# Expert weights split on ScalarE and VectorE, router logits inside attention, one register load per sorted tile, weights moved in 2 KB pieces

## The reference

```python
x = _layernorm(x + attn(x))                  # 16 heads of 16, ONE k and v head of 16, causal
x = _layernorm(x + xattn(x, ctx, ctx))       # 32 query heads and 8 k/v heads of 8, not causal
probs = softmax(xf @ gate_w)                 # xf: 2048 x 256, 8 experts
w, idx = top_k(probs, 2); w = w / w.sum(-1)
out = sum over e of comb[:, e] * ((silu(g_e) * u_e) @ expert_down[e])   # g_e, u_e = xf @ expert_gate_up[e], 512 each
x = _layernorm(x + out + base_mlp(x))        # the base MLP has the same shape and runs on every token
```

## Time and profile before

| | us |
|---|---|
| median of 3 runs | 762.73 (762.64 to 770.33) |
| the profiled execution, whole | 764.03 |
| its span, first to last instruction | 762.2 (granted clock 0.957) |

### The profile page before, as it was taken

How to read it: one execution, slowest core, us unless ns; L and a number is a source line. 1 busy time by engine, 2 the same in 40 slices (tenths; PEclk the granted TensorE clock), 3 DMA queues, 4 the chain that set the end, 5 groups by cost and what they waited for, 6 DMA issues and landing times. The chain is left out here.

```text
span 762.2 us, 11308 instructions
## 1 busy us (share of the span) xinstructions
PE 632.4 (83%) x3379; PEld 436.6 (57%) x3379; DVE 476.9 (63%) x972; ACT 307.3 (40%) x657; POOL 224.8 (29%) x223
## 2 busy tenths in 40 slices
PE   3767989898898898899767998997898888998981
PEld 2444435555454545454335876776686776777770
DVE  4578998988888988978762472333333333344286
ACT  2435656655656655565553211222222222223114
POOL 2344653244432244423200002233333333332100
PEclk9989999999999999999997799999999999999997
DMA  8241344413444313342204800015515542110513
GB/s 265 84 152 59 138 138 153 150 65 105 152 139 153 130 65 124 138 145 105 90 14 149 374 0 28 29 53 197 210 42 201 208 152 92 44 47 24 183 39 110
DMA packets 34727, 90.46 MB, mean 119 GB/s; under 512 B 6028, under 2 KB 24975, under 8 KB 33648
## 3 DMA queue, kind: packets, MB, share of 16 engines
q1 hardware_dynamic: 30928, 80.43, 29.5%
q0 software_dynamic: 3744, 9.31, 3.8%
HBM read 56.18 MB, written 34.47 MB: 119 GB/s over the span
## 5 line engine op out<-in xcount | busy, mean ns | idle before, releaser
L1135 ACT ACTIVATE silu<-inner 128x512 f32<-128x512 f32 x55 | 32.9, 598 | 185.4 <-PE inner L1523 135.1
L493 ACT ACTIVATE prob<-scores 128x1024 f32<-128x1024 f32 x96 | 98.2, 1025 | 13.1 <-PE scores L846 7.8
L1296 DVE TENSOR_TENSOR hT<-hiddenT,hT 128x512 fp32r<-128x512 f32 x39 | 27.0, 692 | 111.5 <-ACT hT L1141 111.5
L1113 POOL DMA_INDIRECT chosen_y<-y_rows,to_row x39 | 40.0, 1026 | 161.2 <-DVE y_rows L1311 161.2
L1518 PE MATMUL inner<-weights,sT_hi 128*128 x156 | 69.1, 443 | 20.9 <-issue 20.9
L626 DVE TENSOR_REDUCE max_c<-scores 128x8 f32<-128x1024 f32 x64 | 77.9, 1217 | 5.8 <-PE scores L909 4.3
L919 PE MATMUL scores<-q_c,k_c 128*128 128x512 f32 x128 | 48.0, 458 | 33.3 <-DVE max_s L626 26.9
L390 POOL TENSOR_TENSOR xT_lo<-xT_in,xT_hi 128x256 fp32r<-128x256 f32 x16 | 11.9, 747 | 192.5 <-ACT xT_hi L464 192.5
L1107 POOL DMA_INDIRECT rows<-x,from_row x39 | 38.1, 978 | 91.9 <-DVE from_row L1278 80.4
L933 PE MATMUL sums<-prob,v_c 128*32 128x512 f32 x256 | 63.0, 604 | 0.0
L1519 PE MATMUL inner<-weights,sT_hi 128*128 x156 | 61.8, 396 | 0.0
(11 more groups left out here) (217 smaller groups left out, 1482.1 us busy)
## 6 DMA issues: line engine op xcount, KB each, us to landing
split_w<-halves SPq DMA_DIRECT2D x16, 1536.0 KB, 6.6
weights<-split_w SPq DMA_DIRECT2D x8, 3072.0 KB, 11.2
raw_w<-in_expert_w SPq DMA_DIRECT2D x16, 768.0 KB, 8.1
weights<-chosen_y SPq DMA_DIRECT2D x8, 512.0 KB, 7.4
xT_in<-in_xT SPq DMA_DIRECT2D x16, 128.0 KB, 2.7
x_in<-in_x SPq DMA_DIRECT2D x16, 128.0 KB, 2.4
x<-stream SPq DMA_DIRECT2D x16, 128.0 KB, 1.7
ctxT_in<-in_ctxT SPq DMA_DIRECT2D x16, 96.0 KB, 2.3
```

The lines of the kernel that those rows point to most:

```text
L493: act.activation(prob[:, m, :], scores[:, n, :], ACT.Exp, scale=scale).then_inc(sem[exped], 1)
L1113: pool.indirect_dma_start(out=shared, out_offset=bass.IndirectOffsetOnAxis(ap=to_row[:, j:j + 1], axis=0), in_=y_rows[j % 3][:], in_offset ...
```

## The change

- `w_high` goes from POOL to ACT, in two casts of 768 columns; `w_low` goes from POOL to DVE, one step later than before (delta 1). `store_w` goes one step later too (delta 0).
- `store_w` is two DMAs, one per part; in DRAM the split weights lie in pieces of 512 values (2 KB), and an expert's load is made of 2 KB pieces.
- The logits of a tile are made in attention (`x2_logit`, on PE and a copy on ACT) into an SBUF tile; the 32 matmuls behind the barrier go. `x2_logit` takes a slot of `misc` ahead of `x2_turn`, and the pipeline has one more step at its end.
- A sorted tile has one register load on PE; the other, with the wait for the weights, is POOL's (`go`), between gather and scatter.
- The base weights are split two steps earlier; `y_rows` lies in the memory of `lane_hot`; an expert without rows gets one tile.

```diff
+PIECE = 512
+PIECES = HALF // PIECE
...
-    ("x2_turn", 0, -2),
+    ("x2_logit", 0, -3), ("x2_turn", 0, -2),
...
-    ("s_rsqrt", 0, 1), ("c_read", 1, -1), ("c_rows", 0, 1), ("c_exp", 0, 0), ("s_read", 0, 2),
-    ("c_exp", 1, 0), ("c_turn", 0, 1), ("c_exp", 2, 0), ("c_values", 0, 1), ("s_read", 1, 2),
-    ("c_exp", 3, 0), ("s_rows", 0, 4), ("x2_read", 0, -2),
+    ("s_rsqrt", 0, 1), ("w_high", 0, 2), ("c_read", 1, -1), ("c_rows", 0, 1), ("c_exp", 0, 0), ("s_read", 0, 2),
+    ("c_exp", 1, 0), ("c_turn", 0, 1), ("c_exp", 2, 0), ("c_values", 0, 1), ("w_high", 1, 2), ("s_read", 1, 2),
+    ("c_exp", 3, 0), ("s_rows", 0, 4), ("x2_logit", 0, -3), ("x2_read", 0, -2),
...
-    ("c_ln", 0, -2), ("c_rows", 0, 1), ("c_den", 0, -1), ("c_den", 1, -1), ("c_out", 0, -1), ("c_out", 1, -1),
-    ("s_max", 1, 3), ("c_res", 0, -1), ("s_den", 0, 2), ("c_stats", 0, -1), ("s_out", 0, 2), ("c_max", 0, 1), ("s_bias", 0, 4),
+    ("c_ln", 0, -2), ("w_low", 0, 1), ("c_rows", 0, 1), ("w_low", 1, 1), ("c_den", 0, -1), ("c_den", 1, -1), ("c_out", 0, -1), ("c_out", 1, -1),
+    ("s_max", 1, 3), ("c_res", 0, -1), ("s_den", 0, 2), ("c_stats", 0, -1), ("s_out", 0, 2), ("c_max", 0, 1), ("s_bias", 0, 4), ("w_low", 2, 1),
     ("s_shift", 0, 3),
...
-    ("s_split", 0, 4), ("w_high", 0, 2), ("c_keys", 0, 1), ("w_low", 0, 2), ("w_low", 1, 2),
-    ("x_bias", 0, 2), ("w_low", 2, 2), ("base_split", 0, 2),
+    ("s_split", 0, 4), ("c_keys", 0, 1), ("x_bias", 0, 2), ("base_split", 0, 2),
...
-    ("store_w", 0, 1), ("load_w", 0, 3), ("store_x2", 0, -2),
+    ("store_w", 0, 0), ("load_w", 0, 3), ("store_x2", 0, -2),
...
     "x2_turn": [("x2_read", 1, 1)],
+    "x2_logit": [("x2_logit_read", 1, 1)],
...
-    split = nc.dram_tensor("split_w", (EXPERTS, P, 2, 2, HALF), F32, kind="Internal").ap()
+    split = nc.dram_tensor("split_w", (EXPERTS, 4 * PIECES, P, PIECE), F32, kind="Internal").ap()
...
             def store_w(seq, unit):
                 wait(sp, sem["w_low"], seq, 3)
-                sp.dma_start(split[seq.off // 2, :, :, seq.odd, :], f32(halves[seq.odd][:])).then_inc(split_stored[seq.odd], 16)
+                for part in range(2):
+                    at = PIECES * (2 * part + seq.odd)
+                    sp.dma_start(split[seq.off // 2, at:at + PIECES].rearrange("c p n -> p c n"),
+                                 f32(halves[seq.odd][:, part, :]).rearrange("p (c n) -> p c n", n=PIECE)).then_inc(split_stored[seq.odd], 16)
...
-                sp.wait_ge(split_stored[p], 16 * EXPERTS)
+                sp.wait_ge(split_stored[p], 32 * EXPERTS)
...
-            def w_high(seq, unit):
-
-                p = seq.odd
-                wait_loaded(pool, w_loaded, seq)
-                if seq.off >= 2:
-                    wait_loaded(pool, split_stored, seq.back(2))
-                pool.tensor_copy(halves[p][:, 0, :], raw_w[p][:]).then_inc(sem["w_high"], 1)
-
-            def w_low(seq, third):
-                p, n = seq.odd, HALF // 3
-                wait(pool, sem["w_high"], seq)
-                pool.tensor_tensor(halves[p][:, 1, n * third:n * third + n], raw_w[p][:, n * third:n * third + n],
-                                   f32(halves[p][:, 0, n * third:n * third + n]), ALU.subtract).then_inc(sem["w_low"], 1)
...
-                k = seq.off - 3
+                k = seq.off - 1
...
+            def w_high(seq, unit):
+                p, n = seq.odd, HALF // 2
+                wait_loaded(act, w_loaded, seq)
+                if unit == 0 and seq.off >= 2:
+                    wait_loaded(act, split_stored, seq.back(2), 2)
+                act.copy(halves[p][:, 0, n * unit:n * unit + n], raw_w[p][:, n * unit:n * unit + n]).then_inc(sem["w_high"], 1)
+            def x2_logit(seq, unit):
+                n = misc_ring.slot("x2_logit", 0, seq)
+                wait(act, sem["x2_logit"], seq)
+                act.copy(logits[:, seq.off, :], misc[:, n, 0:EXPERTS]).then_inc(sem["x2_logit_read"], 1)
...
+            def w_low(seq, third):
+                p, n = seq.odd, HALF // 3
+                if third == 0:
+                    wait(dve, sem["w_high"], seq, 2)
+                dve.tensor_tensor(halves[p][:, 1, n * third:n * third + n], raw_w[p][:, n * third:n * third + n],
+                                  f32(halves[p][:, 0, n * third:n * third + n]), ALU.subtract).then_inc(sem["w_low"], 1)
...
+            def x2_logit(seq, unit):
+                n = misc_ring.slot("x2_logit", 0, seq)
+                wait(pe, sem["x2_read"], seq)
+                if seq.off == 0:
+                    pe.wait_ge(base_loaded, 48)
+                misc_ring.wait_free(pe, sem, "x2_logit", 0, seq)
+                for k in range(2):
+                    mm = pe.matmul(misc[:, n, 0:EXPERTS], xT2[:, k, S * seq.off:S * seq.off + S], gate[:, k, :], start=(k == 0), stop=(k == 1))
+                mm.then_inc(sem["x2_logit"], 1)
...
-        y_rows = three("y_rows", [P, D])
...
+        y_rows = [lane_hot[:, 16 + 4 * p:20 + 4 * p, :].rearrange("p a b -> p (a b)").bitcast(F32) for p in range(3)]
...
-                sp.dma_start(f32(weights[:, e % RING]), split[e]).then_inc(weights_loaded[e], 16)
+                sp.dma_start(f32(weights[:, e % RING]).rearrange("p a k (c n) -> p (a k c) n", n=PIECE), split[e].rearrange("c p n -> p c n")).then_inc(weights_loaded[e], 16)
...
+            def go(j):
+                if j == 0:
+                    pool.wait_ge(sem["tile_set"], 1)
+                needed = pool.value_load(tile_ready[0:1, j:j + 1], min_val=1, max_val=EXPERTS)
+                pool.wait_ge(sem["weights_ready"], needed)
+                pool.sem_inc(sem["go"], 1)
             for j in range(AHEAD):
                 gather(j)
+            go(0)
+            go(1)
             for j in range(SORTED):
                 if j + AHEAD < SORTED:
                     gather(j + AHEAD)
+                if j + 2 < SORTED:
+                    go(j + 2)
                 scatter(j)
...
-                dve.wait_ge(sem["logits_full"], 1)
-                then(dve.tensor_reduce(stat["max"][:], logits, AX.X, ALU.max))
-                then(dve.tensor_tensor(gates["shifted"][:], logits, each(stat["max"][:]), ALU.subtract))
+                then(dve.tensor_reduce(stat["max"][:], logits[:], AX.X, ALU.max))
+                then(dve.tensor_tensor(gates["shifted"][:], logits[:], each(stat["max"][:]), ALU.subtract))
...
-                then(dve.tensor_scalar(small["padded"][:], small["padded128"][:], -TO_128, None, ALU.add))
+                then(dve.tensor_scalar(small["padded"][:], small["padded128"][:], -TO_128, float(P), ALU.add, ALU.max))
...
-            for t in range(B):
-                for k in range(2):
-                    mm = pe.matmul(logits[:, t, :], xT2[:, k, P * t:P * t + P], gate[:, k, :], start=(k == 0), stop=(k == 1))
-            mm.then_inc(sem["logits_full"], 1)
...
                     slot_of[j] = pe.value_load(tile_slot[0:1, j:j + 1], min_val=0, max_val=RING - 1)
-                    needed = pe.value_load(tile_ready[0:1, j:j + 1], min_val=1, max_val=EXPERTS)
+                    pe.wait_ge(sem["go"], j + 1)
...
-                if h == 0:
-                    pe.wait_ge(sem["weights_ready"], needed)
```

More of the change, by code:

```diff
@@ L206, in decoder_layer @@
         gate = sb("gate", [P, 2, EXPERTS])
+        logits = sb("logits", [P, B, EXPERTS])
         base_loaded = both.enter_context(nc.semaphore("base_loaded"))
@@ L211, in decoder_layer @@
         attention(nc, x, xT, ctx, ctxT, wqkvT, bqkv, woT, bo, consts, stream, ident, eps, base_gu, base_down,
-                  gate_w, gate, base_hi, base_lo, base_dn, base_loaded, base_split, expert_w, split, split_stored, xT2, x2, x2_stored)
-        experts(nc, split, split_stored, routing, x2, x2_stored, shared, stream, xT2, ident, eps, gate, base_hi, base_lo, base_dn,
+                  gate_w, gate, base_hi, base_lo, base_dn, base_loaded, base_split, expert_w, split, split_stored, xT2, x2, x2_stored,
+                  logits)
+        experts(nc, split, split_stored, routing, x2, x2_stored, shared, stream, xT2, eps, ident, logits, base_hi, base_lo, base_dn,
                 base_loaded, base_split, out)
 def attention(nc, x, xT, ctx, ctxT, wqkvT, bqkv, woT, bo, consts, stream, ident, eps, base_gu, base_down,
-              gate_w, gate, base_hi, base_lo, base_dn, base_loaded, base_split, expert_w, split, split_stored, xT2, x2, x2_stored):
+              gate_w, gate, base_hi, base_lo, base_dn, base_loaded, base_split, expert_w, split, split_stored, xT2, x2, x2_stored,
+              logits):
     score_ring, prob_ring, sum_ring, misc_ring = rings()
@@ L438, in c_keys @@
                 ins.then_inc(sem["ctx_k_set"], 1)
-            run(pool, POOL_ORDER, dict(s_split=s_split, x_bias=bias, c_keys=c_keys, w_high=w_high, w_low=w_low,
-                                       base_split=split_base))
+            run(pool, POOL_ORDER, dict(s_split=s_split, x_bias=bias, c_keys=c_keys, base_split=split_base))
         @block.scalar
```

(7 more changed lines are left out.)

10 lines of the change are left out of this document (5 added, 5 removed).

## The result

The changed kernel takes 703.9 us (median of 4 runs, 703.5 to 706.9), the kernel before 766.5 us in the runs beside it (median of 4, 762.6 to 772.1). The ratio is 0.919, 95% interval 0.911 to 0.926. The profiled execution of the kernel before, with a mean granted clock of 0.957, is one of its faster ones: its runs beside the experiments lie between 761.2 us (clock 0.959) and 775.9 (0.930), half of them above 768.

The account below looks back on a forecast made before the run. In attention neither DVE nor PE was given a lead, DVE's stalls beside POOL being the removable part. From 764.0, −19, −11.2, −14.8 and −8.1 gave 710.9; less 1.3 for the median, 710 us, range 694 to 738.

Parts of the forecast that it names:

- What bounds attention: Attention: DVE stalls beside POOL cost 3.3 us a step, three subtractions on DVE 2.0; net −1.3, step 22.4 to 21.1.
- the prediction's own signs of being wrong: Stores over 8 us, `w_high` waiting for `split_stored`, subtractions over 0.8, or a step PE-bound at 20.5 or more, DVE idle.
- attention's sum of −19: Attention: −17 from thirteen full steps, −4 from the earlier base split, +2 for first loads and last logits.
- the −4 for the base weights' split: Attention: two steps where POOL splits base weights have the worst stalls; moving them into the pipeline's filling saves 4 us.
- Behind the barrier, −11.2: Behind the barrier: 13.79 us of logits go, then `xg_lo` holds PE's start; first use moves from 427.45 to 416.2.
- Register load, −14.8: Sorted tiles: one of two loads leaves PE, saving 0.41 of a 0.58 us gap in 36 places.
- Gathers, −8.1: Sorted tiles: with 2 KB pieces gathers land in 4 us, so five waits behind weight loads, 8.1 us, go.
- shorter tiles make more gathers late: Sorted tiles: the gathers' better bound, −9, adds to 8.1 what shorter tiles would have added in waits.
- Attention without gain: Rival, chance 0.2: in attention, idle time, PE's added work and ACT's smaller cover cancel the 1.3 a step; 729 us.
- Gathers that stay late: Rival, chance 0.2: in sorted tiles gathers still queue behind many pieces, the 8.1 us stay; 718 to 721 us.
- Slow stores: Rival, chance 0.04: 2 KB pieces slow the stores that ACT's `w_high` awaits; 775 at twice the landing, near 860 at three times.
- A late `go`: Rival, chance 0.06: in sorted tiles POOL's `go` waits for weights and holds back scatters, costing the register load's gain; 725 us.

Follow-up runs that it names:

- e5: The changed kernel with the router logits again as 64 passes behind the barrier, the split staying on ACT and DVE: 701.1 us, ratio to before 0.917.
- e11: The changed kernel once more, unaltered, on the same chip as the last two experiments: 704.9 us, ratio to before 0.919.
- e3: The changed kernel with `w_high` and `w_low` on POOL again and the store back at its old place: 746.0 us.
- e10: The changed kernel with both the split of the weights on POOL again and the logits behind the barrier: 745.8 us.
- e1: The changed kernel with both register loads of a sorted tile on PE again and no `go` on POOL: 723.9 us, ratio to before 0.945.
- e6: The changed kernel with the split weights in DRAM in the old layout, loads in runs of 24 KB, two stores kept: 720.1 us, ratio 0.938.
- e4: The changed kernel with `w_low` alone on POOL, behind `c_keys`, and `w_high` still on ACT: 710.4 us.

## Why the prediction was right, and where it was not

It said 710 us, 694 to 738; 703.9 was measured.

- **What bounds attention.** That DVE's small instructions stood still beside POOL's two-input operations, and that the subtractions would cost less than that, was right: 0.16 us each and 0.68 us. The step of 21.2 us was forecast as 21.1, but by DVE's sum. PE is what holds it there, so one of the prediction's own signs of being wrong came true, a step bound by PE at 20.5 or more with DVE idle (18.6 of 21.2 busy). The step without logits is 20.5 (e5), close to the 20.05 of PE's work that the prediction named as a floor: DVE's idle time shrank along with its work, so −1.9 a step and not −1.3.
- **The step that failed: attention's sum of −19.** The total, −21.2, is near, and its parts are not, so that it fits is in part luck. The ten full steps gave −22.0 where 1.3 each had been reckoned for thirteen of them, the filling −7.2 and the drain +8.0 where a few us had been put down for both. Left out was the clock: PE's wait of 1.89 us was counted as a wait only. In five steps it was followed by some 3.4 us at 1.2 GHz, 1.3 to 1.6 us more each, and with the wait those went as well. The mean clock of 0.96 of the whole part, beside 1.00 in the one step that was taken for all, stood in the earlier trace rows. The changed kernel has 0.96 over the part as well, but its low stretches lie in the drain and behind the barrier. In the drain that is part of the +8.0: 70.0 us at a mean of 0.88, 68.6 at 0.94 in e11, 62.0 at 1.00 before. What the rest is was not shown. Against a kernel that keeps everything else of the change, moving the split is worth 42 to 45 us (e3, e10), and 33.6 against the kernel before without the logits (e5), not 19. The sum has one more wrong reading, the −4 for the base weights' split: POOL split them at 91.1 to 94.7 and 113.0 to 116.6 us, the longest `t_s` (2.54) is at 41.8 and the two longest `x1` (2.08 and 2.07) are at 111.2 and 321.3, so none of them stands beside it; what does is a `c_ln` of 2.46 us.
- **Behind the barrier, −11.2.** Measured −10.5 to `from_row`, and for the reason given. But it was entered as a gain, with 0.43 us of PE's time a tile as its cost, and that cost was put aside because DVE was taken for the bound. The cost is 0.7 a step and 5 in the drain, 12.4 in all (e5). As a part of the change it brings nothing that can be measured.
- **Register load, −14.8.** Mis-sized: 20.4, and 22.9 without the waits for rows that the shorter tiles bring back. The mechanism was right; the share of the gap that is one load was guessed at 0.41 of 0.58 and is all of it.
- **Gathers, −8.1.** Taken alone, right: e1, which has the pieces and two loads, has sorted tiles of 219.2 us against 227.5, −8.3. That the number fits is partly luck: their landing was forecast at 4 us and is 7.7 there at most (7.4 in the changed kernel), and the wait is not gone. 1.2 us are left with the long tiles of e1, so the waits gave 6.9; most of the other 1.4 is the low clock behind one of before's waits, which the prediction did not count. With tiles 0.64 us shorter 3.7 us are left, and 6.1 in e11. The bound "shorter tiles make more gathers late" was seen and not followed: without pieces the faster tiles would have given back 8.2 of 20.4 us (e6, 215.3 against 227.5 − 20.4 = 207.1).
- **Rivals.** Attention without gain: no. Gathers that stay late: in part, 3.7 of 8.1 (6.1 in e11). Slow stores: no; a store of half the bytes lands in 5.3 us and ACT waited for one once, 0.3 us, too little to matter, though the prediction had named any such wait as a sign of being wrong. A late `go`: PE waits for it nowhere in the views.

## What to carry to other kernels

When a wait of the bound engine goes, look at the granted clock behind it, not only at the wait, and take the mean of all steps rather than a clean one. When one change takes an engine off the path, price the others against the engine that is then the bound: a piece of work that is "hidden" on PE is paid in full once PE is it. Undo the parts one at a time and in pairs, since their worth depends on each other (pieces were worth 8.3 us with long tiles and 16.5 with short ones).

## What the runs showed of the hardware that was not expected

- PE stood idle for 1.9 us once in a step in which it otherwise waits 0.5 us at most. In four of eight such steps of before, and in all nine of e10, the granted clock fell to 0.50 within about 1 us of its restart and stayed there for 3.4 us; in the other four it held, and once after a wait of 3.1 us. In e4, with 0.5 us of idle time in its place, it never fell.
- A second and a third register load on PE cost 0.60 and 0.59 us a tile, with no overlap, and with one alone the gap is 0.3 us over all tiles.
- The slowest gather beside weight loads of 3 MB lands in 9.9 us with runs of 24 KB, 7.4 to 7.7 with pieces of 2 KB and 7.5 with 1 KB. By the Trainium skill ("DMA: Bandwidth & Descriptors", section "Queues, rings and completion order") an engine changes queues only at the end of a packet, which may hold several descriptors; that 1 KB brings nothing over 2 KB would fit it, and no run here shows the packets.
